# First loads in order of need, zero products on TensorE while it waits, tile 0 in halves, and GpSimd's sums of exponentials moved behind tile 11

## The reference

```
h = layer_norm(x);  q, k, v = h @ wq, h @ wk, h @ wv          # 4 heads of 256
q = softmax(q * scale, axis=-1)                               # over the 256 of a head
k = softmax(k * scale, axis=-2)                               # over all 4096 rows
context = einsum('bhnd,bhne->bhde', k, v)
attn = einsum('bhnd,bhde->bhne', q, context)
x1 = x + attn @ wo + bo
x2 = x1 + gelu(layer_norm(x1) @ w_ff1 + b_ff1) @ w_ff2 + b_ff2
x3 = layernorm(x + (x2 @ w_d + b_d))
out = layernorm(x3 + (silu(x3 @ wg.T) * (x3 @ wu.T)) @ wd.T)
```

## Time and profile before

| | us |
|---|---|
| median of 3 runs | 1382.55 (1382.44 to 1386.41) |
| the profiled execution: its time | 1383.19 |
| the profiled execution: span of the slowest core | 1381.6 |
| spans of the eight cores | 1378.5 to 1381.6 |
| TensorE busy | 1353.3 (98%) |
| VectorE busy | 557.7 (40%) |
| ScalarE busy | 390.3 (28%) |
| GpSimd busy | 190.4 (14%) |

### The profile page before, as it was taken

The page is one execution under the profiler, slowest core; times in us unless marked ns, Lnnn a source line. Parts: engine busy times, 40 slices in busy tenths (PEclk is TensorE's granted clock), DMA queues, the critical chain, the costliest instruction groups (busy, mean ns, idle before and its releaser), DMA issues.

```text
span 1381.6 us, 17723 instructions; the slowest of 8 cores (1378.5 to 1381.6 us)
## 1 busy us (share of the span) xinstructions
PE 1353.3 (98%) x6484; PEld 626.9 (45%) x6484; DVE 557.7 (40%) x1020; ACT 390.3 (28%) x720; POOL 190.4 (14%) x103
## 2 busy tenths in 40 slices
PE   5999999999999999999999999999999999999997
PEld 4444444454444444444444444444444444444443
DVE  5765675256812111211123555632222222223566
ACT  4632333113763221122113445321111111111225
POOL 1522211217182000000100222200000000000000
PEclk9999999999999999999999999999999999999999
DMA  9844443298747830312101455460030100100113
GB/s 200 208 97 102 93 99 61 45 185 226 136 81 135 155 61 1 61 23 39 51 11 39 103 111 153 99 198 1 0 122 0 62 1 0 62 1 0 61 62 122
DMA packets 104773, 112.95 MB, mean 82 GB/s; under 512 B 90480, under 2 KB 90736, under 8 KB 102000
## 3 DMA queue, kind: packets, MB, share of 16 engines
q1 hardware_dynamic: 101664, 77.68, 22.0%
q0 software_dynamic: 2736, 33.56, 13.0%
q10 hardware_dynamic: 288, 0.59, 0.1%
HBM read 108.66 MB, written 8.39 MB: 85 GB/s over the span
## 4 chain that ended last, share of the span: by engine, by line
PE 93%; DMA 2%; DVE 2%; ACT 2%; issue 1%; DVEq 0%; ACTq 0%; SPq 0%; POOLq 0%
PE P L926 28%; PE P L1113 22%; PE P L897 16%; PE P L413 9%; PE P L471 5%; PE P L835 4%; PE P L1022 4%; PE P L696 2%; PE P L1079 2%; DMA xsA<-xkv 2%; DVE XHa L297 1%; DMA S<-wk 1%; ACT HT L391 1%; PE P L752 0%; PE P L727 0%
## 5 line engine op out<-in xcount | busy, mean ns | idle before, releaser
L926 PE MATMUL P<-S,GB 128*128 128x512 bf16 x1776 | 389.5, 379 | 0.0
L1113 PE MATMUL P<-T,S 128*128 128x512 bf16 x1408 | 305.7, 379 | 0.0
L933 DVE TENSOR_TENSOR R<-R,P 128x1024 f32<-128x1024 f32 x111 | 135.4, 1220 | 386.3 <-PE P L926 386.3
L926 PEld LDWEIGHTS P<-S,GB 128*128 128x128 bf16 x1776 | 173.7, 98 | 209.6
L897 PE MATMUL P<-T,S 128*128 128x512 bf16 x1024 | 225.1, 379 | 0.2 <-ACT GB L909 0.2
L1113 PEld LDWEIGHTS P<-T,S 128*128 128x128 bf16 x1408 | 137.8, 98 | 166.1
L413 PE MATMUL P<-S,HT 128*128 128x512 bf16 x704 | 156.8, 379 | 3.0 <-DVE HT L326 1.7
L897 PEld LDWEIGHTS P<-T,S 128*128 128x128 bf16 x1024 | 100.2, 98 | 121.2 <-issue 0.7
L909 ACT ACTIVATE GB<-P,pv 128x512 bf16<-128x512 f32 x128 | 86.0, 685 | 242.2 <-PE P L897 242.2
L1123 ACT ACTIVATE sl<-P 128x512 bf16<-128x512 f32 x88 | 52.4, 596 | 361.1 <-PE P L1113 355.1
L1126 DVE SCALAR_TENSOR_TENSOR GB<-sl,P 128x512 bf16<-128x512 bf16 x88 | 60.4, 687 | 208.5 <-PE P L1113 206.4
(11 more groups left out here) (114 smaller groups left out, 862.5 us busy)
## 6 DMA issues: line engine op xcount, KB each, us to landing
S<-wff POOLq DMA_DIRECT2D x8, 2048.0 KB, 17.3
xsA<-xkv SPq DMA_DIRECT2D x16, 512.0 KB, 6.3
xsB<-xkv SPq DMA_DIRECT2D x16, 512.0 KB, 4.2
R<-xkv SPq DMA_DIRECT2D x16, 512.0 KB, 10.4
xsD<-xkv SPq DMA_DIRECT2D x16, 512.0 KB, 4.1
y<-R SPq DMA_DIRECT2D x14, 512.0 KB, 2.7
S<-wgT SPq DMA_DIRECT2D x2, 2048.0 KB, 15.0
S<-wuT SPq DMA_DIRECT2D x2, 2048.0 KB, 14.9
```

Source lines behind the costliest of these rows:

```text
L926: tk = p.pe(lambda e, hc=hc, hf=hf: e.matmul(P[pr][:, hf * 512:(hf + 1) * 512], gb[:, hc * 512 + tile * 128:hc * 512 + tile * 128 + 128], ...
L933: t_R[i] = p.ve(lambda e: e.tensor_tensor(rrow(i), rrow(i), P[pr][:, :], ALU.add), tk, t_R[i])
L1113: tk = p.pe(lambda e, c=c, hc=hc, b=b, sw=sw: e.matmul(bank(b), S[sw][:, c * 1024 + hc * 128:c * 1024 + hc * 128 + 128], T[:, c * 2048 + t ...
```

## The change

- The first loads: wk0 now waits for x0, x2 for wk0, and x4 for x2. The others wait as before.
- A constant for the logarithm is written by VectorE (epsc), so that the statistics and the loading of ScalarE's table no longer wait for the parameters pv.
- TensorE multiplies a zeroed tile: 12 products at the start, 4 after the statistics of tile 0, 3 after its reciprocal deviation.
- Tile 0 is normalised in two halves, and its first transposes wait for the first half only. K_quarter(0,0) stands ahead of T_tile(1).
- The second half of tile 8 is copied by VectorE.
- GpSimd's adds no longer stand at each K. `sums(n)` issues the adds up to tile n - 1; it is called first at i = 11, with two further tiles at each turn until it has caught up.
- A2 and A1 of tiles 10 to 15 stand one ahead of K and one behind G at i = 8 to 10. K of tiles 11, 13 and 15 goes to PSUM pair 3. wq is asked for at the end of i = 10, after the transposing of tile 14.

```diff
-        t_xn[j] = p.ve(lambda e: e.tensor_scalar(xh(j), xs(j), mu, rs,
-                                                 ALU.subtract, ALU.mult), t, *ring)
+        if j == 0:
+            t_xn0[0] = p.ve(lambda e: e.tensor_scalar(
+                xh(0)[:, 0:512], xs(0)[:, 0:512], mu, rs, ALU.subtract, ALU.mult), t)
+            t_xn[0] = p.ve(lambda e: e.tensor_scalar(
+                xh(0)[:, 512:1024], xs(0)[:, 512:1024], mu, rs, ALU.subtract, ALU.mult), t)
+        else:
+            t_xn[j] = p.ve(lambda e: e.tensor_scalar(xh(j), xs(j), mu, rs,
+                                                     ALU.subtract, ALU.mult), t, *ring)
...
-                if hb == 0 or j >= 8:
+                if hb == 0 or j >= 9:
...
-        acc_add(i)
+
+    n_acc = [0]
+
+    def sums(upto):
+
+        while n_acc[0] < upto:
+            acc_add(n_acc[0])
+            n_acc[0] += 1
...
-    p.se(lambda e: e.activation(ln[:, 191:192], pcol(CEPS, 0), AF.Ln), t_pv)
+    warm = at("warm", 512, BF16, oXA)
+    t_warm = p.ve(lambda e: e.memset(warm[:, :], 0.0))
+    t_eps = p.ve(lambda e: e.memset(epsc, EPS))
+    p.se(lambda e: e.activation(ln[:, 191:192], epsc, AF.Ln), t_eps)
+
+    def busy(n, tok):
+
+        for k in range(n):
+            p.pe(lambda e: e.matmul(bank(5), warm[:, 0:128], warm[:, :], start=True, stop=True),
+                 tok if k == 0 else None)
...
     load_x(0)
     load_x(1)
-    load_wk(0)
-    load_x(2, t_x[0])
+    load_wk(0, t_x[0])
     load_wk(1, t_x[1])
-    load_x(3, t_wk[0])
+    load_x(2, t_wk[0])
     load_wk(2, t_x[2])
-    load_x(4, t_wk[1])
+    load_x(3, t_wk[1])
+    load_x(4, t_x[2])
     load_wk(3, t_x[3])
     load_x(5, t_wk[2])
     load_x(6, t_x[4])
     load_x(7, t_wk[3])
 
+    busy(12, t_warm)
     A1(0)
+    busy(4, t_agg[0])
+    busy(3, t_ln[0][0])
     A2(0)
     t_b1 = p.ve(lambda e: e.tensor_copy(b1b[:, :], pv[:, B1:B1 + 8]), t_pv)
     T_tile(0, 1)
+    K_quarter(0, 0)
     A2(1)
     T_tile(1, 2)
-    K_quarter(0, 0)
     K_quarter(1, 0)
...
         K_quarter(i, 3)
-        acc_add(i)
...
-        if i == 6:
-            t_wq = load_w("gpsimd", 1, wq_d, 0, t_x[14])
-        K(i, i % 2 if i < 8 else 0)
+
+
+        if 8 <= i < 11:
+            A2(2 * i - 6)
+            A1(2 * i - 5)
+        if i < 8:
+            K(i, i % 2)
+        else:
+            K(i, 3 if 11 <= i < 16 and i % 2 == 1 else 0)
+        if i >= 11:
+            sums(min(2 * (i - 10), i + 1))
...
-
         if 8 <= i < 11:
-            for j in (2 * i - 6, 2 * i - 5):
-                A2(j)
-                A1(j + 1)
+            A2(2 * i - 5)
+            A1(2 * i - 4)
+        if i == 10:
+            t_wq = load_w("gpsimd", 1, wq_d, 0, t_xt[14])
...
         K(i, 0 if i % 2 == 0 else 1)
+        sums(i + 1)
```

More of the change, by code:

```diff
@@ L203, in build_nc @@
     ident = pv[:, 66:130].bitcast(BF16)
+    epsc = ln[:, 186:187]
     b1col = lambda c: b1b[:, c:c + 1]
@@ L280, in build_nc @@
     t_ln = [None] * 32
+    t_agg = [None] * 32
+    t_xn0 = [None]
     def A1(j):
         t, o = ln_stats(xs(j), t_x[j])
+        t_agg[j] = t
         t = p.se(lambda e: e.activation(ln[:, o + 17:o + 18], ln[:, o + 13:o + 14], AF.Ln,
-                                        bias=pcol(CEPS, 0)), t, t_pv)
+                                        bias=epsc), t, t_eps)
         t = p.se(lambda e: e.activation(ln[:, o + 15:o + 16], ln[:, o + 17:o + 18], AF.Exp,
@@ L382, in T_tile @@
                     pb[:, k * 128:(k + 1) * 128], xh(j)[:, c * 128:(c + 1) * 128], ident),
-                    *([t_xn[j], free[b], t_cb] if k == 0 else []), sig=(k == 3))
+                    *([t_xn0[0] if j == 0 and hb == 0 else t_xn[j], free[b], t_cb]
+                      if k == 0 else []), sig=(k == 3))
             if stats is not None and hb == (1 if j < 5 else 0):
```

## The result

The changed kernel is slower: ratio to the kernel before 1.0112 (95% interval 1.0087 to 1.0137), lowest times 1399.3 against 1382.4 us. The medians of 9 runs (1401.5, and 1386.4 before) hold disturbed executions, which the ratio leaves out, and some executions hold a single late core that widens the interval, so I compare the experiments by the eight cores of one profiled execution each: T5, G4 and the mean span. The profiled execution took 1400.74 us, its cores 1393.2 to 1399.2 (before 1378.5 to 1381.6); the mean over the cores went from 1379.7 to 1396.1, +16.4. I forecast 1380.6 and a range up to 1391.5.

A forecast was written before the change was run, and what follows sets the result against it. Loads were taken to bound the first stretch, VectorE held up by GpSimd the second. A gain of 4.1 us up to K12's end less 2.2 for loads gave -1.9 net, 1380.6 us; range 1376.5 to 1391.5.

The forecast's parts named there:

- Step 5: Scalings of tiles 12 to 15 beside 12 unpaused adds: two scalings per add, a 2.1 us stall in K12.
- rival A: Same scalings: only one gets through per add, +8.4 us in all, 1391; chance 0.22.
- Step 4: Late wq: costs nothing itself; the transposing DMA of tile 15 it meets takes 3.0 to 4.9 us.
- Step 2: New order of the first loads: engines run dry, tile 5's transposes come 2.2 us later, bounds 0 and +4.
- rival C: First stretch: loads cost 4 us and TensorE falls to its lower level; net about +0.5, 1383; chance 0.10.
- Step 1: Start: tile 0 in halves, logarithm constant without pv and zero products, costed at nothing either way.
- Step 3: Tile 5's transposes to K12: moved sums, fourth PSUM pair and split A2/A1 remove waits; without a stall K12 ends 47.95 us on.
- I cost that at nothing: Behind the scalings: VectorE's two normalisations and two additions to G fit within 13.8 us, costing nothing.

The follow-up runs named there:

- e1_wq_early: Changed kernel with wq asked for at i = 6 behind x14, as before, and the first add waiting for transposed tile 14: ratio 1.0073.
- e8_wq_after_15: Changed kernel with wq waiting for the transposed tile 15 instead of 14: ratio 1.0032.
- e9_paced: Changed kernel with wq behind transposed tile 15 and each add called at turn i waiting for the exponential of tile i: ratio 1.0009.
- e12_wq_early_best: Changed kernel with old load order, adds at each K, no zero products, and wq asked for at i = 6 behind x14: ratio 0.9976.
- e7_no_zeros: Changed kernel with old load order, adds at each K, no zero products, and wq behind transposed tile 15: ratio 0.9965.
- e4_before_wq_late: Kernel before with only wq moved, to the end of i = 10 behind transposed tile 14: ratio 1.0171.
- e11_wq_halves: Kernel before with wq late in two halves, the first behind transposed tile 14, the second behind transposed tile 15: ratio 1.0058.
- e5_loads_only: Kernel before with only the order of the first loads changed as in the change: ratio 1.0022.

## Why the prediction was wrong

**Step 5 failed, and it alone would turn the sign.** "So two scalings go through per add" rested on 0.07 us against 0.15 between recorded starts. Both numbers were right (79.37 stands 0.08 us behind the end of the add before it); the inference was not: a VectorE operation is recorded as begun before it has the ports, so that its recorded start doesn't tell who comes next. With adds back to back the cycle is one scaling, 2.27 us. I had this as rival A at 0.22, with G4 at T5 + 60.3; in e1_wq_early, where the scalings begin 1.8 us sooner than I had put them, T5 + 57.2 was measured, 3.6 behind before where I had 4.1 ahead of it. The row against me I had quoted myself: the add of 82.21 that went ahead of a queued scaling. A queue of twelve in a row was the new state, and one single add in the old trace couldn't show who comes next; there rival A deserved the larger chance. The backlog costs 5.5 us where it begins behind the second scaling (e8_wq_after_15 against e9_paced) and 9.2 where all eight meet it (e1_wq_early against e9_paced, G4 behind T5; that wq is early in the one and late in the other doesn't move G4, which is at T5 + 49.6 in e12_wq_early_best and e7_no_zeros alike).

The page "SBUF — State Buffer" of the Trainium skill, "Who interferes with whom", has an exclusive lock for whole instructions; the runs agree with that (a scaling of 0.3 us stands 2.34). Of two queues against each other these runs show: in turn, one each.

**Step 4 failed by the size of a term, the largest of all.** I let the transposing DMA of tile 15 take 4.9 us beside wq, the worse median of the earlier trace rows. It took 15.7 on the slowest core and landed with wq. Nothing in the trace of before had a transposing DMA issued behind a whole 2 MB cast transfer; 4.9 was the nearest row and not a bound, and I didn't name the other end, wq's own landing time, 17.4 us in the trace of before. Issued at T5 + 35.4, as I had it, the transposing DMA would by that have landed at T5 + 52.8, and with the measured 15.7 at 51.1 (the scalings began at 51.0 on core 2, 49.6 in the mean). W costs 11.2 us (after against e8_wq_after_15), 12.5 alone (e4_before_wq_late). The page "DMA: Bandwidth & Descriptors" of the Trainium skill says under "Queues, rings and completion order" that an engine alternates between queues packet by packet. The trace agrees: 52 packets of wq and 51 of the transposing DMA from 84 to 88 us. wq has 144 packets in all and the transposing DMA 1056, so in turn by packets most of the small ones get through only when the large ones have ended. e11_wq_halves fits that: 61 of them pass beside wq's first half up to 86 us, 995 in the 2 us that follow. Why the first small packet goes only at 81.6, 6.6 us behind its issue, no run shows. My step 4 cites "35 us later, nothing" for wq itself: right, and beside the point. What mattered was whom it passed in the DMA engines.

**Step 2 had the mechanism and half of the price.** Forecast +2.2 with 4 as the upper bound, measured +4.1 alone (e5_loads_only) and +4.5 in after. Two terms were off. x0 isn't faster by holding wk0 back: its statistics begin at 6.4 in the mean before and at 6.5 after, on the slowest cores at 7.7 and 7.8, where I had 5.5. So on core 2 all the following came 1.5 us or more later than I had worked out: x2 at 20.5 instead of 17 to 17.7, x3 at 24.0 instead of 22.5, x5 at 34.3 instead of 32.8. In the mean of the cores x5 came 3.7 us later than before (29.1 and 32.9), and that is most of the 4.5. The rest is that TensorE, not x5, was the last link on seven of the eight cores, at the lower level. Core 2:

```profile
20.53 0.69 DVE L221 BATCH_NORM_STATS2 ln<-xsA 128x6 f32<-128x512 f32 x1 [4.36 <-DMA xsA<-xkv]
...
24.79 5.59 PE L469 MATMUL P<-S,HT 128*128 128x256 bf16 x32
...
30.67 5.40 PE L469 MATMUL P<-S,HT 128*128 128x256 bf16 x48
```

TensorE had waited 3.10 us for tile 2. Then 32 products take 5.59 us, where at the upper level 48 take 5.40. From tile 2 (transposed at 23.99) to T5 there is no wait: 15.9 us of products on end. That is rival C's mechanism; it had a chance of 0.10.

**Step 1 held.** The zero products bring nothing: the clock had fallen again by K of tile 0 (8 quarter products in 1.87 us at 15.23), and on core 2 they even stood in front of tile 0's transposes, which began at 12.48 though the first half was normalised at 10.73. They cost nothing either, T5 is 32.8 without them and 33.4 with them, the one late core included.

**Step 3 held exactly, and it is the one with a gain.** Without the losses of steps 4 and 5, T5 to G4 is 48.0 us (e9_paced), against 47.95 worked out and 53.6 before; tile 15 is normalised at T5 + 34.3 in after, where I had 34.5. Most of it doesn't need the adds moved: 49.5 with the adds at their K.

**"I cost that at nothing"** for VectorE's debts behind K12 held for after (no wait of TensorE between G4 and the later stages beyond 0.2 us), and failed for the paced version, where K of tile 16 waits up to 2.6 us.

The account of the 16.4 us: loads +4.5, wq +11.2, backlog +5.5, less the 5.6 (53.6 to 48.0) of step 3, is 15.6; 0.8 for the lower level in G4. The shares of wq and the backlog hang on the order in which they are taken away, since a late transposing DMA lets part of the adds run off ahead of the scalings: the wq share first is 7.5 (after against e1_wq_early), and 9.2 is then left for the backlog. Only their sum, 16.7, is fixed.

## What to carry to other kernels

Work moved in program order runs when its queue is free, not where it stands: a batch of old work whose inputs are long there comes as one block, and here the scalings of the other engine then went at one for each add. Before a large transfer is put anywhere, list the small ones that will be issued just behind it; a load that is needed late can be asked for early. And when a step's price has only a distant row, take the length of the whole neighbour as the other end of the bound.

## What the runs showed of the hardware

- Back-to-back GpSimd adds and VectorE scalings in bf16 from SBUF to SBUF alternate strictly: a 0.3 us operation every 2.27 us.
- A transposing DMA of 0.26 MB issued 0.5 us behind a 2 MB cast transfer landed after 15.7 us, 0.9 behind that transfer; behind half of it VectorE's wait was 4.5 us shorter (13.58 and 9.13).
- The packets of the two queues went in turn, 52 of 16 KB and 51 of less than 512 bytes in 4 us. So the transfer of many small packets ended last: 982 of its 1056 went after all but 23 of the other's 144.
- After a wait of 11.75 us TensorE's next 16 products took 6.07 us instead of 3.61.
- The first tile of x came no sooner when 1 MB of wk beside it was held back: its statistics began at 6.4 us in the mean with it and at 6.5 without.
